# Sixteen-head attentions of a fused gated cross-attention stack: scores in 32-row tiles over four banks, a four-tile loop, bias terms moved

## What is computed

```python
x = x + jnp.tanh(g_xattn[0]) * _L0_xattn_ref(_layernorm(x, axis=-1), ctx_1024, ctx_1024, L0_xattn_igate_w, L0_xattn_igate_b, L0_xattn_fgate_w, L0_xattn_fgate_b, L0_xattn_norm_w)
...
x = x + jnp.tanh(g_xattn[1]) * _L1_xattn_ref(_layernorm(x, axis=-1), ctx_1024, ctx_1024, mask_BxS_ik0, L1_xattn_wq, L1_xattn_bq, L1_xattn_wk, L1_xattn_bk, L1_xattn_wv, L1_xattn_bv, L1_xattn_wo, L1_xattn_bo)
...
x = x + jnp.tanh(g_xattn[2]) * _L2_xattn_ref(ctx_1024, ctx_1024, _layernorm(x, axis=-1), mask_Bx1xSxS2_ik1, L2_xattn_W_out, L2_xattn_b_out)
```

## Time and profile before

| what | us |
|---|---|
| median of three runs | 4728.21 (4727.75 to 4728.28) |
| the profiled execution, its own time | 4727.55 |
| its span (first to last instruction) | 4725.8 |
| PE busy, share of the span | 3853.4, 82% |
| DVE busy | 2978.3, 63% |
| ACT busy | 1879.4, 40% |
| POOL busy | 1471.9, 31% |

### The profile page before, as it was taken

One profiled execution on the slowest core, in us unless ns is written; L12 is line 12 of the kernel. 1 busy time (PEld: TensorE's weight loads), 2 busy tenths in 40 slices (PEclk: granted clock), 3 DMA queues, 4 the chain that ended last, 5 costly groups with the idle time before them and its releaser, 6 DMA issues. The chain is left out here.

```text
span 4725.8 us, 92359 instructions
## 1 busy us (share of the span) xinstructions
PE 3853.4 (82%) x30155; PEld 2452.7 (52%) x30155; DVE 2978.3 (63%) x6417; ACT 1879.4 (40%) x3789; POOL 1471.9 (31%) x1831
## 2 busy tenths in 40 slices
PE   5775599998999597015998699795999898999987
PEld 5443254444677332014666466563666654666644
DVE  3898511111777769885776667565777654777744
ACT  1332222222666416332454122363666522666521
POOL 0775100000333005431543000002776501776600
PEclk9998699999999698557998699756999998999998
DMA  2110000000000000002111000200000000000000
GB/s 77 42 40 23 25 0 0 0 0 5 11 11 11 7 0 0 0 0 49 35 36 37 0 0 0 90 0 18 10 9 8 9 0 16 10 9 8 5 5 36
DMA packets 113835, 75.94 MB, mean 16 GB/s; under 512 B 48852, under 2 KB 109400, under 8 KB 112600
## 3 DMA queue, kind: packets, MB, share of 16 engines
q1 hardware_dynamic: 112312, 74.57, 5.5%
q10 hardware_dynamic: 1440, 0.34, 0.0%
HBM read 62.34 MB, written 4.19 MB: 14 GB/s over the span
## 5 line engine op out<-in xcount | busy, mean ns | idle before, releaser
L2129 POOL TENSOR_TENSOR la_turned<-la_turned,la_sines 128x1024 f32<-128x1024 f32 x128 | 301.8, 2358 | 695.5 <-DVE la_sines L2055 695.5
L750 DVE TENSOR_TENSOR l0f_y<-A,l0f_s 128x512 f32<-128x512 f32 x16 | 11.1, 692 | 463.4 <-PE A L717 463.4
L2123 POOL TENSOR_TENSOR la_scaled<-la_turned,la_rlen 128x1024 f32<-128x1024 f32 x128 | 243.6, 1903 | 17.1 <-POOL la_rlen L2116 13.7
L1869 PE MATMUL A<-l1f_wT,l1f_down_oq 128*128 128x128 f32 x384 | 54.6, 308 | 227.2 <-DVE l1f_down_oq L1830 227.1
L1015 POOL TENSOR_TENSOR l1x_kx<-l1x_kT,head_of 128x512 f32<-128x512 f32 x128 | 130.8, 1042 | 263.3 <-ACT l1x_kT L1116 263.3
L1006 POOL COPY l1x_vd<-half 128x16 f32<-128x16 f32 x4 | 0.6, 213 | 650.4 <-POOLq L47 650.4
L2353 ACT ACTIVATE gg_gate<-B,gg_b 128x512 f32<-128x512 f32 (+1 forms) x96 | 65.9, 686 | 278.2 <-PE B L2384 278.2
L2025 ACT ACTIVATE la_sq<-A 128x1024 f32<-128x1024 f32 x128 | 131.3, 1025 | 110.4 <-PE A L2175 88.3
L2047 DVE TENSOR_TENSOR la_turned<-A,la_cos 128x1024 f32<-128x1024 f32 x128 | 155.4, 1214 | 30.9 <-ACT la_sq L2025 15.9
L1869 PEld LDWEIGHTS A<-l1f_wT,l1f_down_oq 128*128 128x128 f32 x384 | 51.9, 220 | 231.2 <-DVE l1f_down_oq L1830 216.5
L2009 ACT ACTIVATE la_prob<-la_prob 128x512 f32<-128x512 f32 x128 | 80.7, 630 | 204.0 <-DVE la_prob L2068 204.0
(11 more groups left out here) (441 smaller groups left out, 11046.7 us busy)
## 6 DMA issues: line engine op xcount, KB each, us to landing
memory_ctx<-in_ctx SPq DMA_DIRECT2D x128, 64.0 KB, 2.2
l2x_ctx<-in_ctx SPq DMA_DIRECT2D x128, 64.0 KB
X<-in_x SPq DMA_DIRECT2D x4, 1024.0 KB, 7.4
gates_ctxT<-in_ctxT SPq DMA_DIRECT2D x16, 256.0 KB, 2.8
memory_ctxT<-in_ctxT SPq DMA_DIRECT2D x64, 64.0 KB, 1.7
l1x_ctxT<-in_ctxT SPq DMA_DIRECT2D x64, 64.0 KB, 1.8
l2x_raw<-in_l2x_mask SPq DMA_DIRECT2D x2, 2048.0 KB
l2x_ctxT<-in_ctxT SPq DMA_DIRECT2D x64, 64.0 KB, 1.8
```

Of the source, the lines that this page charges most:

```text
L2123: pool.tensor_tensor(by_head(scaled), by_head(turned), spread_heads(rlen[j % 2][:], W3), ALU.mult)\
L2129: pool.tensor_tensor(turned[j % 2][:], turned[j % 2][:], sines[j % 2][:], ALU.add)\
```

## The change

Per tile, in both attentions:

- The scores become eight products of 32 contracted rows, 64 output rows and 256 columns: one for each quarter of the features (four heads) and each sequence. Each quarter writes a bank of its own, so one tile's scores fill all four banks of `A`, now single-buffered. `qx` with its zeros is gone (`qT` is one plain tile), `kx` repeats four times.
- Turned probabilities move to `B[0]`; mix, turned outputs, inputs and projections to the two banks of `B[1]`.
- Loops run over four tiles (`steps4`, `at4`, moved up in the file), with counters shared by all buffers. `mix` and what follows it come a tile later than before (lags -2 and -3 in place of -1 and -2; DVE's `update` -4 in l1x), context tiles and `vd` have four buffers.
- In l1x the values are made with 64 columns per product, without the zeros between, ACT copies them in place of DVE, and their bias isn't added there. Both biases go into `shift_by`, computed once (tanh of the gate times the bias row); POOL adds it to each X tile (`move_x`) once the tile is normalized. The one-row product of the output bias is gone.
- The layer-2 mask is loaded once per tile rather than twice, in 256-byte pieces, in the program's first compute stage (`gates`), ahead of that stage's context loads on SP's queue; DVE converts it in the stage `decay`.

```diff
+                by_pair = d["l2x_mask"].rearrange("q (t b) k -> b q t k", b=2)
+                for b in range(2):
+                    sp.dma_start(m.mask_raw[b * S:b * S + S], by_pair[b]).then_inc(m.mask_in, 16)
...
+                dve.wait_ge(m.mask_in, 32)
+                dve.tensor_scalar(m.masks[:], m.mask_raw[:], 0, -1e20, ALU.is_equal, ALU.mult)
...
+        s_banks = m.A_all[:].rearrange("p (r c) -> p r c", r=R)
+        s = s_banks[:, :, 0:E * S]
+        s_heads = s.rearrange("p r (e k) -> p r e k", e=E)
+        turned_p, mixes, inputs = m.B[0], m.B[1][:, 0:CH], m.B[1][:, CH:2 * CH]
+        out = mixes[:, 0:G * NW].rearrange("p (h w) -> p h w", h=H)
+        if projected:
+            turned_o, y_out = mixes[:, G * NW:G * NW + P], inputs[:, P:2 * P]
+        else:
+            turned_o, y_out = inputs[:, P:2 * P], inputs[:, 2 * P:3 * P]
+        x_in, k_out, v_out = inputs[:, 0:P], inputs[:, P:2 * P], inputs[:, 2 * P:3 * P]
+        n_masked = 2 + 7 * projected
...
+                def spread_k(it, j):
+                    if projected:
+                        pool.wait_ge(k_set, done(it, j))
+                    else:
+                        pool.wait_ge(ctx_in[j], it * 16 + 16)
+                    pool.wait_ge(scored, done(it, j, 2))
+                    k = (kT[j % 2] if projected else ctxT[j])[:].rearrange("p (b k) -> p b k", b=2)
+                    pool.tensor_tensor(kx[j % 2][:], k[:, :, None, :].broadcast_to([P, 2, E, S]),
+                                       head_of_4[:, None, :, None].broadcast_to([P, 2, E, S]), ALU.mult)\
+                        .then_inc(spread, 1)
...
+                def move_x(it, j):
+                    t = it * 4 + j
+                    pool.wait_ge(normed_x, done(it, j))
+                    pool.sem_inc(seen, 1)
+                    pool.tensor_tensor(m.X[:, t, :], m.X[:, t, :], shift_by[:], ALU.add).then_inc(moved, 1)
...
+                def step(it, j):
+                    at4(it, j, 1, spread_k)
+                    if not projected:
+                        at4(it, j, 1, apart)
+                    at4(it, j, 2, move_x)
+                steps4(pool, step)
...
+                def update(it, j):
+                    t = it * 4 + j
+                    dve.wait_ge(out_done, done(it, j))
+                    dve.wait_ge(moved, done(it, j))
+                    if projected:
+                        dve.wait_ge(q_set, ahead(it, j, 5))
+                    dve.scalar_tensor_tensor(m.X[:, t, :], y_out, m.tanh_g[:, gate_at:gate_at + 1], m.X[:, t, :],
+                                             ALU.mult, ALU.add).then_inc(added, 1)
+                def measure(it, j):
+                    t = it * 4 + j
+                    dve.wait_ge(added, done(it, j))
+                    dve.bn_stats(m.S6[:, t, :], m.X[:, t, :])
...
+                dve.tensor_scalar(shift_by[:], x_in, m.tanh_g[:, gate_at:gate_at + 1], None, ALU.mult)\
+                   .then_inc(masked, 1)
+                def step(it, j):
+                    if projected:
+                        at4(it, j, -4, update)
+                    at4(it, j, 0, shift)
+                    if not projected:
+                        at4(it, j, -3, update)
+                    at4(it, j, -2, outputs)
+                    at4(it, j, -4 if projected else -3, measure)
...
+                def copy_x(it, j):
+                    act.wait_ge(v_made, done(it, j))
+                    act.wait_ge(q_made, done(it, j, 2))
+                    act.copy(xnT[j % 2][:], x_in).then_inc(copied, 1)
...
                 def keep_v(it, j):
-                    dve.wait_ge(q_set[j], past(it + 1))
-                    dve.wait_ge(mixed[j], past(it))
-                    v = F[j][:, 2 * P:4 * P].rearrange("p (b g u w) -> p b g u w", b=2, g=E, u=2)
-                    b_v = bv[:].rearrange("p (g u w) -> p g u w", g=E, u=2)
+                    act.wait_ge(v_made, done(it, j))
+                    act.wait_ge(mixed, done(it, j, 4))
                     for u in range(2):
                         r = slice(u * S, u * S + S)
-                        last = dve.tensor_tensor(vd[j][r, :, :, u, 0:W], v[r, :, :, u],
-                                                 b_v[r, None, :, u].broadcast_to([S, 2, E, W]), ALU.add)
-                    last.then_inc(values[j], 1)
...
+                        last = act.copy(vd[j][r, :, :, u, 0:W], v_out[r].rearrange("p (b g w) -> p b g w", b=2, g=G))
+                    last.then_inc(values, 1)
...
+                def exps(it, j):
+                    by = scale[:, bass.ds(it * 4 + j, 1)] if projected else float(P) ** -0.5
+                    act.wait_ge(shifted, done(it, j))
+                    act.activation(prob[j % 2][:], prob[j % 2][:], ACT.Exp, scale=by).then_inc(exped, 1)
+                def set_q(it, j):
+                    act.wait_ge(q_made if projected else turned, done(it, j))
+                    act.wait_ge(scored, done(it, j, 2))
...
+                        act.wait_ge(out_done, done(it, j, 5) if not isinstance(it, int) else max(done(it, j, 5), BEFORE))
+                        act.activation(qT[j % 2][:], x_in, ACT.Identity, bias=bq[:]).then_inc(q_set, 1)
...
+                def step(it, j):
+                    at4(it, j, -3, copy_o)
+                    if not projected:
+                        at4(it, j, 2, set_q)
+                    at4(it, j, -1, copy_p)
                     if projected:
-                        at(it, j, 1, set_q)
-                    at(it, j, 2, copy_x)
+                        at4(it, j, 2, copy_x)
+                        at4(it, j, 2, set_k)
+                        at4(it, j, 2, keep_v)
+                    at4(it, j, 0, exps)
                     if projected:
-                        at(it, j, 2, set_k)
-                    at(it, j, 0, exps)
-                steps(act, step)
+                        at4(it, j, 2, set_q)
...
+                def scores(it, j):
+                    pe.wait_ge(shifted, done(it, j, 1))
+                    if not projected:
+                        for r in range(R):
+                            pe.matmul(s[:, r], m.ident_bf[:], repeat_heads(m.masks[:, it * 4 + j, :], E),
+                                      start=True, stop=False)
+                    pe.wait_ge(spread, done(it, j))
+                    pe.wait_ge(q_set, done(it, j))
+                    for r in range(R):
+                        for b in range(2):
+                            rows_of, c = slice(r * 32, r * 32 + 32), slice(b * S, b * S + S)
+                            last = pe.matmul(s[c, r], qT[j % 2][rows_of, c], kx[j % 2][rows_of, b],
+                                             start=projected, stop=True)
+                    last.then_inc(scored, 1)
...
+                def turn_p(it, j):
+                    pe.wait_ge(exped, done(it, j))
+                    pe.wait_ge(p_copied, done(it, j, 1))
+                    p = prob[j % 2][:].rearrange("p h k -> p (h k)")
...
                 def turn_x(it, j):
-                    pe.wait_ge(normed_x[j], past(it + 1))
+                    pe.wait_ge(normed_x, done(it, j))
+                    pe.wait_ge(q_set, done(it, j, 1))
+                    pe.wait_ge(added, done(it, j, 6) if not isinstance(it, int) else max(done(it, j, 6), BEFORE))
+                    pe.transpose(x_in, xn[j % 2][:], m.ident[:]).then_inc(turned, 1)
+                def make_kv(it, j):
+                    pe.wait_ge(ctx_in[j], it * 16 + 16)
+                    pe.matmul(k_out, wk[:], ctxT[j][:], start=True, stop=True)
+                    for b in range(2):
+                        for u in range(2):
+                            last = pe.matmul(v_out[u * S:u * S + S, b * S:b * S + S], ctxT[j][:, b * S:b * S + S],
+                                             wv[:].rearrange("p (g u w) -> p g u w", g=G, u=2)[:, :, u],
+                                             start=True, stop=True)
+                    last.then_inc(v_made, 1)
+                def project_q(it, j):
+                    pe.wait_ge(copied, done(it, j))
+                    pe.wait_ge(values, done(it, j))
+                    pe.matmul(x_in, wq[:], xnT[j % 2][:], start=True, stop=True).then_inc(q_made, 1)
...
+                def mix(it, j):
+                    pe.wait_ge(values, done(it, j))
+                    pe.wait_ge(o_copied if projected else o_done, done(it, j, 1))
+                    pe.wait_ge(p_copied, done(it, j))
+                    for g in range(G):
+                        for b in range(2):
...
+                    last.then_inc(mixed, 1)
...
+                def project_o(it, j):
+                    pe.wait_ge(o_copied, done(it, j))
+                    pe.wait_ge(values if projected else q_set, ahead(it, j, 5))
+                    pe.wait_ge(added, done(it, j, 1))
+                    pe.matmul(y_out, oT[j % 2][:], wo[:], start=True, stop=True).then_inc(out_done, 1)
...
```

(38 more changed lines are left out.)

348 lines of the change are left out of this document (142 added, 206 removed).

## The result

The median is 4562.58 us (4560.73 to 4564.11, four runs) against 4728.24 before (four runs too): a ratio of 0.9649, 95% interval 0.9632 to 0.9666. That is 165.7 us less, where 190 were forecast; the time lies inside the range of 4490 to 4625. The profiled execution has a span of 4561.6 us against 4725.8, 164.2 less, and TensorE's mean granted clock is 0.892 against 0.895.

A forecast was written before the change was run, and what follows sets the result against it. PE was taken to set the period in l1x and l2x, DVE right under it. l1x -98.9, l2x -75.0, start of l2x -27 and gates +11 sum to -189.9 us: 4538, range 4490 to 4625.

The forecast's parts named there:

- low bound: Scores on PE: 3.44/8 = 0.43 us a tile, all eight array places at work and no cost for changing tile shape.
- rival of pairs: Scores on PE: only two products overlap, 1.91 + 0.20 us instead of 0.74; total 4652; chance 0.08.
- the ring as named: l2x: norm to next norm through mix, output, update and measure, about 4.2 to 4.3 us; period taken as 4.35.
- chain C: l1x: turned probabilities, their copy, copy_x, set_k, value copies, query product, output, scores, turned outputs, back; 4.34, with crossings 4.4 us.
- Chain A: l1x: subtraction, exponentials, query step, update, reduction, subtraction; 4.23 us and three crossings, so 4.3 to 4.5.
- single-bank rival: A and B banks are single; one more link in chain C or Chain A gives l1x 5.2, l2x 5.0; 4626; chance 0.12.
- Gates: Start of the program: the mask load in 256-byte pieces ahead of the context tiles costs +11 us, span +7 to +21.
- Decay: Stage decay: the mask conversion, 2.2 us, hides in DVE's 3.16 us wait for ACT, so 0; without that cover 2.2.
- The clock: l1x and l2x: PEclk stays at 1.00 in both windows, though PE would hold only 3.86 of 4.45 us in l1x.
- slow rival: l1x and l2x fall to the 1.2 GHz level: PE about 7.2 and 6.6 us a tile, +125, 4853; chance 0.05.
- DVE's operations: Both stages: forecast wrong if POOL's move_x or contention over operands makes them longer, as both periods stand on DVE's floor.
- POOL's added pass: move_x, one more pass over X per tile on POOL: estimated 1.0 us, hidden, POOL at 3.0 and 3.8 us.

The follow-up runs named there:

- the run above: In l2x, project_o was issued ahead of mix on PE, against the changed kernel: 4545.37 us, l2x period 4.02.

## Why the prediction was right, and where not

**What bounds it, and that PE would stop bounding: right.** Scores fell from 1.72 to 0.62, forecast 0.74. All eight places work, not 3.2 of four: a group behind another costs the low bound of 0.43. The 0.19 more of a single group is close to the 0.20 that I had put down for the two changes of tile shape. The rival of pairs (1.91) is refuted by both numbers.

**l2x: right, by its mechanism.** Forecast 4.35, measured 4.33, and the ring as named: moving one of its steps gave 0.31 a tile. Its steps in the trace after:

```profile
2253.53 0.49 PE L1293 MATMUL B<-l2x_wo,l2x_oT 128*128 128x128 f32 x2
2254.19 0.35 DVE L1124 SCALAR_TENSOR_TENSOR X<-B,tanh_g,X 128x128 f32 x1 [0.53 <-PE B L1293]
2255.71 0.32 PE L1261 MATMUL B<-ident,l2x_xn 128*128 128x128 f32 x1 [0.21 <-DVE l2x_xn L199]
2255.87 1.04 PE L1254 MATMUL B<-ident,l2x_prob 128*128 128x128 f32 x8
2256.83 1.11 PE L1284 MATMUL B<-l2x_vd,l2x_pT 128*64 128x18 f32 x32
2257.88 0.49 PE L1293 MATMUL B<-l2x_wo,l2x_oT 128*128 128x128 f32 x2
```

Output product to update 0.66, update to turned input 1.52, turned input 0.16, turned probabilities 0.96, mix 1.05: 4.35. That the number came out to 0.02 is in part luck. The prediction names the ring but writes out none of its terms, and it kept DVE at 4.24 us a tile as the floor, though it said that this might shrink. DVE has 223.28/61.2 = 3.65 in the window after, with the norm at 345 ns where it was 728, and the run above went to 4.02.

**l1x: the step that failed is the size of chain C.** I wrote 4.34 and 4.4 with crossings; it is 4.79, and 4.88 with the loop. Term by term:

| step of chain C | forecast | measured | what made it |
|---|---|---|---|
| turned probabilities to `copy_x` | 1.98 | 1.98 | |
| `copy_x` to the values | 0.56 | 0.71 | 0.42 of work and 0.29 of waiting for the mix, which was in no term |
| values to the query product | 0.53 | 0.70 | 0.15 is the crossing to PE |
| query and output product | 0.42 | 0.62 | see below |
| scores | 0.74 | 0.62 | all eight places work |
| turned outputs | 0.11 | 0.16 | |
| crossings of the whole ring | 0.06 | | they stand in the steps above |

The query and output product and the scores together are 0.08 more. The change of tile shape ahead of the scores, which I had counted with them, seems to show with the output product: it holds PE for 0.33 here and for 0.23 in the run with the scores ahead (1354.55), where turned outputs follow it. I had taken the values' step and the query product at their distance in a full pipeline, though here PE starts the query product from rest. The turning of the loop, 0.09 a tile on average, was in no term either. Chain A, forecast at 4.3 to 4.5 with exponentials of 1.06 (they take 1.15 in l1x), closes at 4.58 and waits on C. The prediction's own span for l1x, 4.1 to 4.8, did not hold 4.88; the range for the whole did, because it was wide and the other terms held. l1x is 27 us off, where the sum of all pieces is 26 off.

**One sign was wrong, and would have misled.** DVE's idle time was to be under 0.5 us a tile, ahead of `update` if chain A binds and ahead of the reduction if chain C does. It is 1.04, ahead of `update`, and chain C binds: what waits longest is not what sets the period.

**The single-bank rival** (0.12) has something of the truth: it foresaw rings lengthened by a link more than counted, 5.2 in l1x. The missing link was not the mix's length (0.96), but the wait for its end (0.29).

**Gates: right** at 12.7 for 11. The Trainium skill ("DMA: Bandwidth & Descriptors", Specifications) wants at least 512 bytes per transfer for the full rate. It gives no factor there for shorter ones; the prediction's twice the time is an estimate, 256 being half of 512. The traces agree that pieces of 256 bytes are slower, but not with my factor: they added 3.3 us to 9.1.

**Decay: right**, the conversion (2.29 at 116.14) is followed by 0.97 of idle time, and nothing of it appears between `gates` and l1x: with the load moved but the conversion in place l1x starts at 1189.5, against 1189.6 before.

**The clock: right in the main** that it stays. With PE busy 83% of l1x, ten turned tiles in each period, it held 1.00 from 1214.8 to the end of the loop. But this isn't firm: the last section shows l1x loops that fell to the 1.2 GHz level for single tiles. By the Trainium skill's rule on transposes ("TensorE: Matmul & The Clock Gate", Part 4) the slow rival would have been likelier. No run here has a stage that goes slow as a whole, and whether the turned tiles have a part in the single ones is not shown.

**DVE's operations** got no longer, as feared at the prediction's end, but shorter: the norm 368 ns for 498 in l1x, 345 for 728 in l2x. Why is open; leaving out `move_x` doesn't change it. POOL's added pass takes 0.46, where 1.0 was estimated, and is hidden as forecast.

## What to carry to other kernels

When a change takes the bounding engine's work away, list every ring of waits that returns to its start one tile later, and add its steps at their length from rest: start of one to start of the next across engines, not the distance in a full pipeline. Then look for links that are buffers, not work. A longer idle time need not be in the ring, and a shorter one can be; test it by moving one step, and when nothing moves, look in the trace for the second ring before calling the first one refuted. A load that has to be early is best put where the queue sleeps and the engines have other work.

## What was not expected of the hardware

Exponentials of 128x1024 take 1.15 us with a scale that is a column of numbers (l1x) and 1.06 with a constant one (l2x); no run changes the scale alone.

Single tiles of over 6 us turn up in the middle of the l1x loop in six of the twelve traces of changed kernels, at one to three places in each, and each place is a stretch in which TensorE's granted clock is at its lower level. Without POOL's pass, the stretch ahead of such a tile, the stretch itself, and a row of PE in it:

```profile
1360.00:1376.00 16.00, 12.96 (x228) 10.74 (x236) 11.92 (x25) 12.90 (x28) 4.02 (x4) 1.00 0.06 16
1376.20:1379.60 3.40, 3.40 (x30) 2.67 (x16) 2.79 (x3) 1.09 (x3) 0.00 (x0) 0.50 0.00 0
```

```profile
1376.98 1.92 PE L1254 MATMUL B<-ident,l1x_prob 128*128 128x128 f32 x8
```

The turned probabilities take 1.92 for 1.04, and the period 6.64. Ahead of the fall PE was busy 81% of the time, as in the tiles of the changed kernel that didn't fall. The two tiles of over 7 us at the start, with the long pieces and with the output ahead of the mix, belong to it too: the clock rose to 1.00 there at 1220.5 and 1223.5, and at 1214.8 in the changed kernel. In the kernel before, where PE never rests, the whole loop from the first reduction on stood at 1.00. Each such place costs some 1.6 us. That PE's new rests open the door to it is suggested by this, not shown: one execution of each kernel was traced, and what makes the clock fall in one tile and not in the next is open. The four traces with eight tiles per pass have no such place ahead of the last tile.

The 8 us of the eight-tile loop go the same way, and so do the 3.8 behind l2x with the mask's load moved (10 us more at the lower level there). In the eight-tile loop's traced execution the stages between l1x and l2x are 4.7 us longer and those behind l2x 5.4, with 10 and 8.5 us more at the lower level; over the whole span the lower level holds for 993 us there, 988 without POOL's pass and 981 in the changed kernel. That the time went with the clock is read from the traces; why the clock differs in stages whose code is the same is open. Differences under 10 us between kernels were therefore read from the stages, not from the medians.
